# Another order of VectorE's step in layer one's attention, and feed-forward output products inside the feed-forward loop

## The chip, the cores and the metric

The kernel runs on one core of a Trainium2 chip. The metric is the device time of one execution in microseconds; lower is better.

## What is computed

A block of a network on 16 sequences of 32 tokens with 512 channels. First a graph attention over the 512 channels seen as points (two layers, windows of ten neighbours, four orderings), then a state-space mixing layer, then a gated feed-forward with repeated weights and low-rank adapters. The change touches the first layer of the graph attention and the feed-forward:

```python
scores = jnp.einsum('bihd,bjhd->bhij', qh, qh) / np.float32(np.sqrt(headdim))
attn = jax.nn.softmax(scores, axis=-1)
out = jnp.einsum('bhij,bjhd->bihd', attn, qh).reshape(B * N, k, total)
...
h1 = jnp.einsum('oc,bnkc->bonk', W_conv1, g1)
h1 = _lrelu(_instance_norm(h1, (2, 3)))
feats1 = h1.max(axis=-1)
...
def _qlora_linear(x, wq, A, B):
    w = jnp.tile(wq, (1, 4))
    return x @ w.T + (x @ A.T @ B.T) * LORA_SCALING
gate = jax.nn.silu(_qlora_linear(x, w1q, a1, b1))
up = _qlora_linear(x, w3q, a3, b3)
return _qlora_linear(gate * up, w2q, a2, b2)
```

## The kernel before

**Layer one's attention.** `windows_and_attention` builds the windows and then runs `steps(engine, step, T, U)` on each engine: T = 192 steps, a hardware loop whose body is U = 8 steps, with the steps ahead of it and behind it written out. `at(lag)` gives the item that a step handles with that lag, so in step k an engine works on items k-1, k-3 and so on. An item is 15 sub-windows of 3 points. Four items (SL = 4) make a pack, whose values are mixed together. What happens to an item, in order:

- TensorE `scores`: a mask product (L1564), then 15 times two products into `pQ` (L1569, L1571).
- ScalarE copies scores to `small`/`Sc` (L1672) and values to `Vs` (L1678), lag 1.
- VectorE takes the maximum `mx` (L1490), lag 1; GpSimd subtracts it, `Dm` (L1428), lag 1; ScalarE takes the exponential `E` (L1691), lag 2; VectorE sums it, `Z` (L1494), and inverts the sum, `R` (L1503), both lag 3; GpSimd multiplies, `A` (L1435), lag 3; VectorE transposes `A` to `AT` (L1499), lag 4.
- TensorE `mix`: once a pack, lag 5, four centre products (L1589) and 60 small products (L1594) into `pH`; it waits for the transposes of the whole pack.
- ScalarE copies the outputs to `Hs` with their sum (L1685) and squares them (L1697); VectorE takes the maximum over neighbours, `hmax` (L1509), all lag 6, once a pack.

The views name tiles by the memory that they lie in: `QT` is Dm, E or A, `onehot` is Vs, Hs or AT, `small` is Sc. Each engine runs its instructions in the order written. VectorE's order in a step is: maximum of k-1, sum of k-3, transpose of k-4, reciprocal of k-3, and once a pack the maximum over outputs of k-6. GpSimd's is: subtract of k-1, multiply of k-3.

**Feed-forward.** The hidden width is cut into 12 parts (HT), n = 0 to 11. For each n TensorE makes six products of 512 columns (`passes`, L2951), two adapter products of 6 rows (`adapters`, L2958) and then the two `low_rank` products of part n-1 (L2939, L2942). ScalarE makes the silu (L2827), VectorE the product with `up` (L2887), ScalarE its high half in 16 bits (L2831), VectorE its low half (L2892), on which the second `low_rank` product waits. GpSimd adds up the four parts that share a row of the repeated weight, `uf` (L2920); for each of three such sums r (FR = 3) ScalarE and VectorE make the high and low half `uf16` (L2834 and L2899, for r = 2 L2836 and L2901). VectorE also makes the low half of the output weights, `W2` (L2894). Behind the loop the output comes: for each of four blocks of tokens q nine products (three r by three pairs of halves, L2984) and one 4-row product in float32 with `la2` (L2986), then VectorE's `res` (L2907) and the store.

Of the kernel before, what the change touches and what calls it, by code (L numbers as in the profile page):

```python
# [6 lines left out]
F32 = mybir.dt.float32  # L7
# [3 lines left out]
ALU = mybir.AluOpType  # L11
# [1161 lines left out]
def windows_and_attention(nc, io, scratch, layer, O, feats, runs, perm, rank, fixed, W, hmax, stat, field):  # L1173
# [12 lines left out]
    with ExitStack() as ctx:  # L1186
# [143 lines left out]
        def valid(tile):  # L1330

            return tile.rearrange("p (s x) -> p s x", x=32)[:, :, 0:PTS * K]
# [109 lines left out]
        def _(dve):  # L1442
# [40 lines left out]
                                    rows(cen, k, 0, (1, PTS), (0, K), (PTS, 2)), ALU.subtract).then_inc(q_v, 1)  # L1483

            def step(k, at):
                if at(1):
                    (t, _), p = at(1), (k - 1) % ND
                    dve.wait_ge(scores_out, t + 3)
                    dve.wait_ge(shifted, t + 1)
                    v.tensor_reduce(mx[:, p, :], valid(Sc[:, p, :]), X, ALU.max).then_inc(max_ready, 1)  # L1490
                if at(3):
                    (t, _), p = at(3), (k - 3) % ND
                    dve.wait_ge(exped, t + 1 + ND)
                    v.tensor_reduce(Z[:, p, :], valid(E[:, p, :]), X, ALU.add).then_inc(summed, 1)  # L1494
                if at(4):
                    (t, r), k5 = at(4), (k - 4) % U
                    dve.wait_ge(probs, t + 1 + ND)
                    dve.wait_ge(mixed, pack(r, k5) + (RV - NA) // SL + 1)
                    v.transpose(AT[:, k5 % NA, :], A[:, k5 % ND, :]).then_inc(turned, 1)  # L1499
                if at(3):  # L1500
                    (t, _), p = at(3), (k - 3) % ND
                    dve.wait_ge(summed, t + 1)
                    v.reciprocal(R[:, p, :], Z[:, p, :]).then_inc(r_ready, 1)  # L1503
                if at(6) and (k - 6) % SL == SL - 1:
                    (_, r), k6 = at(6), (k - 6) % U
                    q, p = pack(r, k6), k6 // SL % 2
                    dve.wait_ge(copied, q + 3)
                    dve.wait_ge(squared, q + 3)
                    v.tensor_reduce(hmax[:, bass.ds(q * GP, GP)],  # L1509
                                    Hs[:, p, :].rearrange("p (n j) -> p n j", j=K), X, ALU.max).then_inc(hmax_done, 1)  # L1510

            steps(dve, gather_step, B, 4)
            steps(dve, step, T, U)
# [1181 lines left out]
def feed_forward(nc, io, scratch, P, out):  # L2695


    with ExitStack() as ctx:
# [8 lines left out]

        HT = 4 * FR
        LR = 38
        UP = 2.0 ** 10  # L2710
        ident = sb("ident_f", [128, 128])
        w13 = sb("w13_f", [128, 2, FFH])
# [29 lines left out]
        pl = ctx.enter_context(nc.psum_tensor("pl_f", [128, 512], F32))  # L2742
        pg = ctx.enter_context(nc.psum_tensor("pg_f", [128, 2, 512], F32))
        pu = ctx.enter_context(nc.psum_tensor("pu_f", [128, 2, 512], F32))
        i_in = sem("i_in_f")
        w_in = sem("w_in_f")
        a_in = sem("a_in_f")
# [36 lines left out]
        def turned_to(d):  # L2784

            return pt[:, d, :] if d < 2 else pu[:, d - 2, :]

        def u_of(n):

# [19 lines left out]
        @block.scalar  # L2809
        def _(act):  # L2810
            act.wait_ge(var_ready, 1)
            nc.scalar.activation(tmp[:, 0, :], mv[:, :, 1], ACT.Sqrt).then_inc(root_ready, 1)
            act.wait_ge(w_in, 32)
            nc.scalar.activation(W16[:, 0, 0, :], w13[:, 0, :], ACT.Copy, scale=UP).then_inc(w_high, 1)
            nc.scalar.activation(W16[:, 1, 0, :], w13[:, 1, :], ACT.Copy, scale=UP).then_inc(w_high, 1)
            act.wait_ge(b_in, 32)
            nc.scalar.activation(bh[:, :], b13[:, :], ACT.Copy, scale=UP).then_inc(b_high, 1)
            act.wait_ge(xf_ready, 1)
            nc.scalar.activation(X16[:, 0, :], xf[:, :], ACT.Copy).then_inc(x_high, 1)
            act.wait_ge(w2_in, 48)  # L2820
            nc.scalar.activation(A2[:, :, 0:2], a2[:, :, :], ACT.Copy, scale=UP).then_inc(w2_high, 1)
            nc.scalar.activation(W2[:, 0, :, :], w2[:, :, :], ACT.Copy, scale=UP).then_inc(w2_high, 1)
            for n in range(HT):
                act.wait_ge(gu_mm, n + 1)
                if n >= 2:
                    act.wait_ge(u_ready, n - 1)
                nc.scalar.activation(sg[:, n % 2, :], pg[0:FP, n % 2, :], ACT.Silu, scale=1.0 / UP).then_inc(silued, 1)  # L2827
                act.wait_ge(u_ready, n + 1)
                if n >= 2:
                    act.wait_ge(la2_mm, n - 1)  # L2830
                nc.scalar.activation(u16[:, n % 2, 0, :], u_of(n), ACT.Copy).then_inc(u_high, 1)  # L2831
                if n % 4 == 3 and n >= 4:
                    act.wait_ge(uf_ready, 3 * (n // 4))
                    nc.scalar.activation(uf16[:, 0, n // 4 - 1, :], uf[:, n // 4 - 1, :], ACT.Copy).then_inc(uf_high, 1)  # L2834
            act.wait_ge(uf_ready, 3 * FR)
            nc.scalar.activation(uf16[:, 0, FR - 1, :], uf[:, FR - 1, :], ACT.Copy).then_inc(uf_high, 1)  # L2836

        @block.vector
        def _(dve):
# [41 lines left out]
            for n in range(HT):  # L2881
# [8 lines left out]
                if n >= 2:  # L2890
                    dve.wait_ge(la2_mm, n - 1)
                v.tensor_tensor(u16[:, n % 2, 1, :], u_of(n), u16[:, n % 2, 0, :], ALU.subtract).then_inc(u_split, 1)  # L2892
                if n == 5:
                    v.scalar_tensor_tensor(W2[:, 1, :, :], w2[:, :, :], UP, W2[:, 0, :, :], ALU.mult, ALU.subtract)\  # L2894
                        .then_inc(w2_split, 1)
                if n % 4 == 3 and n >= 4:
                    r = n // 4 - 1
                    dve.wait_ge(uf_high, r + 1)
                    v.tensor_tensor(uf16[:, 1, r, :], uf[:, r, :], uf16[:, 0, r, :], ALU.subtract).then_inc(uf_split, 1)  # L2899
# [4 lines left out]
            v.tensor_scalar(la2[:, :], pl[0:4, :], 0.5, None, ALU.mult).then_inc(la2_ready, 1)  # L2904
            for q in range(TT):
                dve.wait_ge(out_mm, q + 1)
                v.scalar_tensor_tensor(res[:, q, :], (pg if q < 2 else pu)[:, q % 2, :], 1.0 / UP, x2[:, q, :],  # L2907
                                       ALU.mult, ALU.add).then_inc(res_ready, 1)

        @block.gpsimd  # L2910
# [13 lines left out]
        def _(pe):  # L2924
# [29 lines left out]
            def adapters(n):  # L2954
# [4 lines left out]
                                            L16[32 * i:32 * i + 6, :], start=False, stop=True)  # L2959
                last.then_inc(gu_mm, 1)  # L2960

            pe.wait_ge(x_split, 1)
            passes(0)
            passes(1)
# [6 lines left out]
            for n in range(2, HT):  # L2971
                pe.wait_ge(u_ready, n - 1)
                passes(n)
                adapters(n)
                low_rank(n - 1)
            low_rank(HT - 1)
            pe.wait_ge(w2_split, 1)
            pe.wait_ge(la2_ready, 1)
            pe.wait_ge(uf_split, FR)
            for q in range(TT):  # L2980
                po = (pg if q < 2 else pu)[:, q % 2, :]
                for r in range(FR):
                    for a, b in ((0, 0), (0, 1), (1, 0)):
                        nc.tensor.matmul(po, uf16[:, a, r, q * 128:(q + 1) * 128], W2[:, b, r, :],  # L2984
                                         start=r + a + b == 0, stop=False)
                nc.tensor.matmul(po, la2[:, q * 128:(q + 1) * 128], b2[:, :], start=False, stop=True).then_inc(out_mm, 1)  # L2986


# [118 lines left out]
```

## Time and profile before

| | us |
|---|---|
| median of three runs | 2203.59 |
| lowest and highest run | 2200.35, 3210.74 |
| the profiled execution | 2203.48 |
| its span in the trace | 2201.7 |

| engine | busy us | share of the span |
|---|---|---|
| TensorE | 1865.4 | 85% |
| VectorE | 1840.4 | 84% |
| ScalarE | 1596.5 | 73% |
| GpSimd | 1071.2 | 49% |

Layer one's attention steps run from about 268 to 676 us of the span, the feed-forward from about 2112 us to its end. The shares above are means over all stages; each stage has another limit, so the stages are read one by one. A row of the timeline gives the start, the duration, the engine, the line and the tiles of an instruction; two instructions of one engine may overlap by some hundredths, so what an instruction costs its engine is read from start to start.

### The profile page before, as it was taken

The page shows a single profiled execution, that of the slowest core. Times are in us where ns is not written, and L with a number is a line of the kernel's source. Part 1 is how long each engine was busy: PE and PEld are TensorE (multiplying, and loading weights), DVE is VectorE, ACT ScalarE, POOL GpSimd, SP SyncE. Part 2 cuts the span into 40 slices and gives each one's busy share as a digit, 9 for nine tenths or more (in the row PEclk, how much of TensorE's full clock was granted, in tenths as well). Part 3 has the DMA queues.
Part 4 walks back from the last instruction along what each step waited for, and adds up shares of the span by engine and source line. Part 5 has one row for each costly group of instructions (what it writes and reads, how often), then busy time and mean ns, then how long its engine had stood idle before and what let it go on. Part 6 is the DMA issues. An engine that isn't in the chain of part 4 may idle for free. (4 is left out here: it accounts for less than half of the span.)

```text
span 2201.7 us, 99587 instructions
## 1 busy us (share of the span) xinstructions
PE 1865.4 (85%) x37653; PEld 1274.8 (58%) x37656; DVE 1840.4 (84%) x3511; ACT 1596.5 (73%) x3296; POOL 1071.2 (49%) x1160
## 2 busy tenths in 40 slices
PE   4876688888885674899999994879999999999957
PEld 2333377777773333899999993424545554554522
DVE  8899889999995996799999996847888888888864
ACT  7899778888886996899999993565554554454432
POOL 1220189999992002687788771003445444544511
PEclk9976699999996666999999996999999999999977
DMA  1157865555551776545545531302222222222110
GB/s 37 37 122 175 187 140 126 121 120 127 119 110 34 177 175 159 108 105 110 108 105 108 110 83 45 92 27 91 82 86 76 81 86 79 83 81 86 48 51 20
DMA packets 434897, 215.53 MB, mean 98 GB/s; under 512 B 301196, under 2 KB 404268, under 8 KB 434681
## 3 DMA queue, kind: packets, MB, share of 16 engines
q1 hardware_dynamic: 431872, 212.24, 40.0%
q10 hardware_dynamic: 2936, 2.18, 0.4%
q8 instruction: 48, 0.79, 0.2%
q14 instruction: 41, 0.33, 0.0%
HBM read 161.35 MB, written 52.86 MB: 97 GB/s over the span
## 5 line engine op out<-in xcount | busy, mean ns | idle before, releaser
L1015 PE MATMUL pQ<-QM,QX 128*128 128x96 f16 x2880 | 299.6, 227 | 1.6 <-issue 1.6
L1013 PE MATMUL pQ<-neigh_lo,QX 128*128 128x64 f16 x2880 | 292.7, 195 | 3.3 <-issue 3.3
L1013 PEld LDWEIGHTS pQ<-neigh_lo,QX 128*128 128x128 f16 x2880 | 276.3, 103 | 3.1 <-issue 3.1
L1015 PEld LDWEIGHTS pQ<-QM,QX 128*128 128x128 f16 x2880 | 274.8, 103 | 2.1 <-issue 2.1
L2656 POOL TENSOR_TENSOR MT<-cb,decay 128x512 f32 (+1 forms) x128 | 174.8, 1386 | 207.7 <-DVE half L2567 152.5
L1571 PE MATMUL pQ<-QM,QX 128*128 128x64 f16 x2880 | 232.0, 206 | 0.0
L1569 PE MATMUL pQ<-neigh_lo,QX 128*128 128x32 f16 x2880 | 227.5, 182 | 0.0
L1569 PEld LDWEIGHTS pQ<-neigh_lo,QX 128*128 128x128 f16 x2880 | 218.9, 103 | 2.8
L1111 POOL TENSOR_TENSOR Dm<-Sc,mx 128x450 f32<-128x450 f32 x192 | 183.1, 954 | 71.5 <-DVE mx L1071 71.5
L1571 PEld LDWEIGHTS pQ<-QM,QX 128*128 128x128 f16 x2880 | 212.4, 104 | 0.3
L1435 POOL TENSOR_TENSOR QT<-QT,R 128x450 f32<-128x450 f32 x192 | 183.0, 953 | 37.1 <-DVE R L1503 28.2
L2624 DVE SCALAR_TENSOR_TENSOR cv_m<-pX,taps_m,cv_m 128x496 f32<-128x496 f32 (+2 forms) x192 | 137.6, 717 | 73.6 <-ACT cv_m L2530 55.9
L1118 POOL TENSOR_TENSOR Ap<-E,R 128x450 f32<-128x450 f32 x192 | 182.9, 952 | 30.6 <-DVE R L1084 29.4
L2671 POOL TENSOR_TENSOR sqsum<-sqsum,sq 128x512 f32<-128x512 f32 x56 | 83.0, 1483 | 231.2 <-ACT sq L2519 231.2
L1428 POOL TENSOR_TENSOR QT<-small,mx 128x450 f32<-128x450 f32 x192 | 182.7, 952 | 13.8 <-DVE mx L1490 13.8
L1148 ACT ACTIVATE Vs<-pQ 128x960 f32<-128x960 f32 x192 | 187.0, 974 | 0.0
L2535 ACT ACTIVATE hid<-cv_m 128x512 f32<-128x512 f32 x64 | 40.3, 630 | 198.3 <-DVE cv_m L2624 198.3
L2431 PE MATMUL pG<-h,W 128*128 128x512 f16 x768 | 178.5, 383 | 4.2 <-DVEq L2560 4.2
L2449 PE MATMUL pO<-Wo,yw 128*128 128x512 f16 x768 | 176.2, 379 | 1.6 <-DVE yw L2614 1.6
L2431 PE MATMUL pX<-h,W 128*128 128x512 f16 x768 | 176.2, 379 | 0.0
L1691 ACT ACTIVATE QT<-QT 128x450 f32<-128x450 f32 x192 | 112.2, 584 | 60.1 <-POOL QT L1428 60.1
L1499 DVE STREAM_TRANSPOSE onehot<-QT 128x480 f32<-128x480 f32 x192 | 129.8, 676 | 26.2 <-PE pH L1594 10.7
(455 smaller groups left out, 5221.9 us busy)
## 6 DMA issues: line engine op xcount, KB each, us to landing
QM<-scratch_q SPq DMA_DIRECT2D x192, 240.0 KB, 2.7
QX<-scratch_q SPq DMA_DIRECT2D x768, 60.0 KB, 2.3
scratch_q<-QT SPq DMA_DIRECT2D x124, 360.0 KB, 5.1
Wo<-in_out_proj SPq DMA_DIRECT2D x64, 256.0 KB, 2.6
Wg<-in_in_proj SPq DMA_DIRECT2D x62, 256.0 KB, 2.7
Wh<-in_in_proj SPq DMA_DIRECT2D x62, 256.0 KB, 2.8
W_s<-in_in_proj SPq DMA_DIRECT2D x20, 256.0 KB, 2.7
CT<-scratch_c SPq DMA_DIRECT2D x192, 11.2 KB, 2.1
```

What stands on the lines that cost most here:

```text
L1013: nc.tensor.matmul(pQ[:, p, u // PB, o + 32:o + BW], qx[u], W["neigh_lo"][:, 0:O], start=False, stop=True, skip_group_check=True)
L1015: last = nc.tensor.matmul(pQ[:, p, u // PB, o:o + BW], qx[u], qm[u], start=False, stop=True, skip_group_check=True)
L1111: nc.gpsimd.tensor_tensor(valid(Dm[:, p, :]), valid(Sc[:, p, :]), mx[:, p, :].unsqueeze(2).to_broadcast([128, SUBS, PTS * K]), ALU.subtrac ...
L1118: nc.gpsimd.tensor_tensor(valid(A[:, p, :]), valid(E[:, p, :]), R[:, p, :].unsqueeze(2).to_broadcast([128, SUBS, PTS * K]), ALU.mult).then ...
L1148: nc.scalar.activation(like(Vs[:, kv % RV, :], O, O), blocks(p, 32, O), ACT.Copy).then_inc(vs_ready, 1)
L1428: nc.gpsimd.tensor_tensor(valid(Dm[:, p, :]), valid(Sc[:, p, :]), mx[:, p, :].unsqueeze(2).to_broadcast([128, SUBS, PTS * K]), ALU.subtrac ...
L1435: nc.gpsimd.tensor_tensor(valid(A[:, p, :]), valid(E[:, p, :]), R[:, p, :].unsqueeze(2).to_broadcast([128, SUBS, PTS * K]), ALU.mult).then ...
L1569: nc.tensor.matmul(pQ[:, p, u // PB, o + 32:o + BW], qx[u], W["neigh_lo"][:, 0:O], start=False, stop=True, skip_group_check=True)
L1571: last = nc.tensor.matmul(pQ[:, p, u // PB, o:o + BW], qx[u], qm[u], start=False, stop=True, skip_group_check=True)
L2431: last = nc.tensor.matmul(out, W16[:, i, quarter, a, d, :], h16[:, b, d, :], start=d + a + b == 0, stop=d == DT - 1 and a == 1)
L2449: last = nc.tensor.matmul(pO[:, q, :], yw[:, k4 % 2, a, q * 128:(q + 1) * 128], Wo16[:, k4 % 2, b, :], start=k4 + a + b == 0, stop=k4 == U ...
L2656: nc.gpsimd.tensor_tensor(MT[:, k1 % 2, h, :, :].rearrange("p q (b i) -> p q b i", b=4), P["cb"][:, bass.ds(r, 1), :, :].rearrange("p g q ...
```

## The change

In layer one's attention VectorE's step gets another order: sum of k-3, maximum of k-1, reciprocal of k-3, once a pack the maximum over outputs, now of k-7, then the transpose of k-4. The maximum over outputs no longer waits for the square. Layer two's attention, a function of its own, stays.

In the feed-forward 24 of the 36 output products (those of r = 0 and 1) move from behind the loop into it, as eight pieces of three: five in the iterations 7 to 11 (`EARLY`), three between the loop and the last `low_rank`. For that the outputs lie in other banks, with one new one, `pr`. The halves of `uf` for r = 0 and 1 are made at n = 5 and 9 instead of 7 and 11, the low half of `W2` at n = 3 instead of 5.

```diff
             def step(k, at):
+                if at(3):
+                    (t, _), p = at(3), (k - 3) % ND
+                    dve.wait_ge(exped, t + 1 + ND)
+                    v.tensor_reduce(Z[:, p, :], valid(E[:, p, :]), X, ALU.add).then_inc(summed, 1)
                 if at(1):
...
                     v.tensor_reduce(mx[:, p, :], valid(Sc[:, p, :]), X, ALU.max).then_inc(max_ready, 1)
                 if at(3):
                     (t, _), p = at(3), (k - 3) % ND
-                    dve.wait_ge(exped, t + 1 + ND)
-                    v.tensor_reduce(Z[:, p, :], valid(E[:, p, :]), X, ALU.add).then_inc(summed, 1)
+                    dve.wait_ge(summed, t + 1)
+                    v.reciprocal(R[:, p, :], Z[:, p, :]).then_inc(r_ready, 1)
+                if at(7) and (k - 7) % SL == SL - 1:
+                    (_, r), k7 = at(7), (k - 7) % U
+                    q, p = pack(r, k7), k7 // SL % 2
+                    dve.wait_ge(copied, q + 3)
+                    v.tensor_reduce(hmax[:, bass.ds(q * GP, GP)],
+                                    Hs[:, p, :].rearrange("p (n j) -> p n j", j=K), X, ALU.max).then_inc(hmax_done, 1)
                 if at(4):
                     (t, r), k5 = at(4), (k - 4) % U
                     dve.wait_ge(probs, t + 1 + ND)
                     dve.wait_ge(mixed, pack(r, k5) + (RV - NA) // SL + 1)
                     v.transpose(AT[:, k5 % NA, :], A[:, k5 % ND, :]).then_inc(turned, 1)
-                if at(3):
-                    (t, _), p = at(3), (k - 3) % ND
-                    dve.wait_ge(summed, t + 1)
-                    v.reciprocal(R[:, p, :], Z[:, p, :]).then_inc(r_ready, 1)
-                if at(6) and (k - 6) % SL == SL - 1:
-                    (_, r), k6 = at(6), (k - 6) % U
-                    q, p = pack(r, k6), k6 // SL % 2
-                    dve.wait_ge(copied, q + 3)
-                    dve.wait_ge(squared, q + 3)
-                    v.tensor_reduce(hmax[:, bass.ds(q * GP, GP)],
-                                    Hs[:, p, :].rearrange("p (n j) -> p n j", j=K), X, ALU.max).then_inc(hmax_done, 1)
...
+        EARLY = {7: (0, 0), 8: (1, 0), 9: (2, 0), 10: (0, 1), 11: (1, 1)}
...
+        pr = ctx.enter_context(nc.psum_tensor("pr_f", [128, 512], F32))
...
+        def out_of(q):
+
+            return (pt[:, 0, :], pt[:, 1, :], pr[:, :], pg[:, 0, :])[q]
...
-                if n % 4 == 3 and n >= 4:
+                if n % 4 == 1 and n >= 4:
                     act.wait_ge(uf_ready, 3 * (n // 4))
                     nc.scalar.activation(uf16[:, 0, n // 4 - 1, :], uf[:, n // 4 - 1, :], ACT.Copy).then_inc(uf_high, 1)
...
-                if n == 5:
+                if n == 3:
                     v.scalar_tensor_tensor(W2[:, 1, :, :], w2[:, :, :], UP, W2[:, 0, :, :], ALU.mult, ALU.subtract)\
                         .then_inc(w2_split, 1)
-                if n % 4 == 3 and n >= 4:
+                if n % 4 == 1 and n >= 4:
...
+            def piece(q, r):
+
+                pe.wait_ge(uf_split, r + 1)
+                for a, b in ((0, 0), (0, 1), (1, 0)):
+                    nc.tensor.matmul(out_of(q), uf16[:, a, r, q * 128:(q + 1) * 128], W2[:, b, r, :],
+                                     start=r + a + b == 0, stop=False)
...
                 adapters(n)
+                if n == 7:
+                    pe.wait_ge(w2_split, 1)
+                if n in EARLY:
+                    piece(*EARLY[n])
                 low_rank(n - 1)
+            piece(2, 1)
+            pe.wait_ge(u_ready, HT - 1)
+            piece(3, 0)
+            piece(3, 1)
             low_rank(HT - 1)
-            pe.wait_ge(w2_split, 1)
-            pe.wait_ge(la2_ready, 1)
-            pe.wait_ge(uf_split, FR)
             for q in range(TT):
-                po = (pg if q < 2 else pu)[:, q % 2, :]
-                for r in range(FR):
-                    for a, b in ((0, 0), (0, 1), (1, 0)):
-                        nc.tensor.matmul(po, uf16[:, a, r, q * 128:(q + 1) * 128], W2[:, b, r, :],
-                                         start=r + a + b == 0, stop=False)
+                piece(q, FR - 1)
+                if q == 0:
+                    pe.wait_ge(la2_ready, 1)
+                po = out_of(q)
                 nc.tensor.matmul(po, la2[:, q * 128:(q + 1) * 128], b2[:, :], start=False, stop=True).then_inc(out_mm, 1)
```

## Rows read from the trace of the kernel before

**Rows 1.** Windows view, attention loop: stretch, us, busy (x instructions), clock, DMA

```profile
core 0: us, PE busy (x) PEld busy (x) DVE busy (x) ACT busy (x) POOL busy (x), PEclk, DMA share, GB/s
315.00:660.00 345.00, 294.26 (x10584) 270.53 (x10584) 322.88 (x713) 289.11 (x672) 312.97 (x336) 1.00 0.57 121
```

**Rows 2.** Timeline of VectorE over one pack: start, duration, engine, line, operation

```profile
453.78 0.68 DVE L1499 STREAM_TRANSPOSE onehot<-QT 128x480 f32<-128x480 f32 x1
454.39 0.21 DVE L1503 RECIPROCAL R<-Z 128x15 f32<-128x15 f32 x1
454.52 0.56 DVE L1509 TENSOR_REDUCE hmax<-onehot 128x450 f32 x1
455.00 0.61 DVE L1490 TENSOR_REDUCE mx<-small 128x15 f32<-128x450 f32 x1
455.52 0.61 DVE L1494 TENSOR_REDUCE Z<-QT 128x15 f32<-128x450 f32 x1
456.05 0.67 DVE L1499 STREAM_TRANSPOSE onehot<-QT 128x480 f32<-128x480 f32 x1
456.64 0.21 DVE L1503 RECIPROCAL R<-Z 128x15 f32<-128x15 f32 x1
...
457.99 0.68 DVE L1499 STREAM_TRANSPOSE onehot<-QT 128x480 f32<-128x480 f32 x1
...
460.05 0.68 DVE L1499 STREAM_TRANSPOSE onehot<-QT 128x480 f32<-128x480 f32 x1 [0.24 <-PE pH L1594]
...
462.01 0.68 DVE L1499 STREAM_TRANSPOSE onehot<-QT 128x480 f32<-128x480 f32 x1
```

**Rows 3.** Timeline of GpSimd in the same pack

```profile
454.76 0.95 POOL L1435 TENSOR_TENSOR QT<-QT,R 128x450 f32<-128x450 f32 x1
455.68 0.95 POOL L1428 TENSOR_TENSOR QT<-small,mx 128x450 f32<-128x450 f32 x1
457.01 0.95 POOL L1435 TENSOR_TENSOR QT<-QT,R 128x450 f32<-128x450 f32 x1 [0.37 <-DVE R L1503]
457.92 0.95 POOL L1428 TENSOR_TENSOR QT<-small,mx 128x450 f32<-128x450 f32 x1
```

**Rows 4.** Waits from 300 to 660 us: total us, times, longest

```profile
ACT QT L1691 <- POOL QT L1428: 56.1, 87, 0.8
PE pH L1594 <- DVE onehot L1499: 28.8, 43, 0.7
```

**Rows 5.** Timeline of ScalarE in the same pack

```profile
456.67 0.58 ACT L1691 ACTIVATE QT<-QT 128x450 f32<-128x450 f32 x1 [0.50 <-POOL QT L1428]
457.15 0.53 ACT L1672 ACTIVATE small<-pQ 128x450 f32<-128x450 f32 x1
```

**Rows 6.** Timeline of TensorE behind the feed-forward loop

```profile
2174.54 4.00 PE L2984 MATMUL pg_f<-W_f,uf_f 115*128 115x512 f16 x9 [1.26 <-DVE la_f L2904]
2178.47 2.07 PE L2986 MATMUL pg_f<-b_f,la_f 4*128 4x512 f32 x2
2180.47 4.02 PE L2984 MATMUL pg_f<-W_f,uf_f 115*128 115x512 f16 x9
...
2196.26 1.12 PE L2986 MATMUL pu_f<-b_f,la_f 4*128 4x512 f32 x2
```

**Rows 7.** Windows view: the feed-forward loop, and the products behind it

```profile
2144.90:2172.20 27.30, 21.84 (x91) 6.76 (x89) 18.84 (x22) 12.68 (x22) 10.14 (x8) 1.00 0.00 1
...
2175.60:2196.10 20.50, 20.50 (x40) 5.81 (x38) 2.07 (x3) 0.00 (x0) 0.00 (x0) 0.50 0.10 38
```

**Rows 8.** Timeline of TensorE in the feed-forward loop, iterations 9 and 11

```profile
2162.18 0.82 PE L2951 MATMUL pg_f<-X_f,W_f 128*128 128x512 f16 x3
...
2163.59 0.39 PE L2958 MATMUL pg_f<-L_f,B_f 6*128 6x512 f16 x1
...
2167.59 0.82 PE L2951 MATMUL pg_f<-X_f,W_f 128*128 128x512 f16 x3
```

**Rows 9.** Source view of L2892: durations in ns, by operands

```profile
L2892 DVE TENSOR_TENSOR u_f<-u_f x9: 1196/1199/1200, 2141.1 to 2171.4; 115x512 f16<-115x512 f32 x9
L2892 DVE TENSOR_TENSOR u_f<-uf_f,u_f x3: 692/693/693, 2139.1 to 2163.7; 115x512 f16<-115x512 f32 x3
```

**Rows 10.** Timeline of VectorE at the end of the feed-forward loop

```profile
2172.56 0.68 DVE L2899 TENSOR_TENSOR uf_f<-uf_f 115x512 f16<-115x512 f32 x1
2173.16 0.68 DVE L2901 TENSOR_TENSOR uf_f<-uf_f 115x512 f16<-115x512 f32 x1
2173.76 0.67 DVE L2904 TENSOR_SCALAR la_f<-pl_f 4x512 f32<-4x512 f32 x1
```

More of the change, by code:

```diff
@@ L2906, in _ @@
                 dve.wait_ge(out_mm, q + 1)
-                v.scalar_tensor_tensor(res[:, q, :], (pg if q < 2 else pu)[:, q % 2, :], 1.0 / UP, x2[:, q, :],
+                v.scalar_tensor_tensor(res[:, q, :], out_of(q), 1.0 / UP, x2[:, q, :],
                                        ALU.mult, ALU.add).then_inc(res_ready, 1)
```

## The prediction

> **What bounds the kernel now.** Only two stages are touched, so I read these and leave the rest alone. First the windows view of the attention loop: 345.00 us hold 168 steps (336 GpSimd instructions, two a step), 2.05 us each. VectorE is busy 322.88 us, GpSimd 312.97, TensorE 294.26, ScalarE 289.11 [rows 1]. No engine is full, so the limit is a ring through several of them, and the timelines show which. From one transpose to the next VectorE takes 2.27, 1.94, 2.06 and 1.96 us, 8.23 a pack [rows 2]. The reader should ask of each length whether VectorE's own work fills it.
>
> The 2.27 is full: transpose 0.61, reciprocal 0.13, maximum over outputs 0.48, maximum 0.52, sum 0.53, from start to start. Without the output maximum the sum is 0.60 + 0.13 + 0.48 + 0.53 = 1.74 (the first reduction of a row costs 0.48, the last 0.53). The other three steps are 0.20 to 0.32 longer than that. What fills them is a ring through GpSimd: the transpose holds the reciprocal back 0.59; the reciprocal at 456.64 lets the multiply start at 457.01, 0.37 later [rows 3]; the multiply lets the next transpose start at 457.99, 0.98 later. 0.59 + 0.37 + 0.98 = 1.94, just the step. The transpose at 460.05, the first of a pack, comes 0.10 later than the ring gives; its row names TensorE, but the buffer that it fills was freed a pack ago, so I keep 0.10 as a fixed cost of that one transpose.
>
> Then the feed-forward's end. Behind the loop TensorE runs four times nine products and a 4-row product in float32: 3.93 + 2.00 us a block [rows 6], from 2174.54 to 2197.4, 22.8 us (the last 4-row product took 1.12). From 2175.60 to 2196.10 it was busy 20.50 of 20.50 us and the granted clock was still 0.50, which is 1.2 GHz; in the loop before it was 1.00 [rows 7]. The clock had fallen while TensorE waited for the last part.
>
> **Attention: the new order.** Nothing is added; each instruction keeps its price. The reciprocal now stands in front of the transpose, so the ring transpose, reciprocal, multiply, transpose is gone: between a reciprocal and the transpose of its product now lie a transpose, a sum, a maximum and a reciprocal, 1.74 us, against the 1.35 that it needs. VectorE's own sum would be 3 x 1.74 + 2.27 = 7.49 a pack.
>
> But the maximum now comes second, and with it the subtract and, behind it on GpSimd, the multiply. Let z be the start of the sum. Maximum at z + 0.48. The subtract starts 0.68 behind the maximum (455.00 to 455.68 [rows 2, 3]; there GpSimd's multiply held it as well, so 0.68 is at most a little too long), so z + 1.16. The multiply follows 0.91 later (454.76 to 455.68 and 457.01 to 457.92 for the other way round, same shape), so z + 2.07, and the transpose of the next step can't start before z + 3.05, in the first of a pack z + 3.15. The transpose is wanted at z + 1.14 of its own step, with the output maximum at z + 1.67, and the next z is 0.60 behind it. So a step that follows one of length x has the length max(1.74, 3.65 - x); with the output maximum max(2.27, 3.65 - x); first of a pack max(1.74, 3.75 - x). The output maximum stands in step 2 of four (lag 7), the first-of-pack transpose in step 0. Going round: step 2 2.27; step 3 max(1.74, 1.38) = 1.74; step 0 max(1.74, 2.01) = 2.01; step 1 max(1.74, 1.74) = 1.74. Sum 7.76 against 8.23, so 0.47 less, 0.117 a step. GpSimd alone would need 4 x 1.82 = 7.28.
>
> What hides the others: ScalarE waits 56.1 us for the subtract [rows 4]; its exponential starts 0.99 behind the subtract, the copy for the maximum 0.48 later [rows 3, 5], and that copy is wanted at the next but one maximum, so 1.16 + 0.99 + 0.48 + about 0.6 = 3.2 against 3.96; the pack's two longer ScalarE steps take 0.5 of the slack and leave some. TensorE waits 28.8 us in 43 packs for the last transpose [rows 4], 0.67 each, besides a wait on ScalarE, so it has a little over the 0.47 that is to be cut. If that cover were gone, it would be TensorE that holds the pack, at 8.23 - 0.67 = 7.56 by this wait alone. The output maximum reads a copy made one ScalarE step earlier and is one step later than before: no wait; the square's wait is dropped and cost nothing in a steady pack. No DMA is moved. Of 48 packs the first four are held by filling and I count 44: 44 x 0.47 = 20.7 us. Bounds: 0, and 44 x 0.74 = 32.6 if only VectorE's sum holds.
>
> By the Trainium skill ("SBUF — State Buffer", Who interferes with whom) a VectorE instruction with two SBUF inputs is blocked by a GpSimd one that reads SBUF, one with a single input is not. The trace agrees for the first: the low half beside GpSimd's sum takes 1199 ns, otherwise 693 [rows 9]. That rule speaks for unchanged prices in the attention.
>
> **Feed-forward.** 24 of 36 products leave the end. What stays per block: three products, 3.93 / 3 = 1.31, and the 4-row one, 2.00, at 1.2 GHz; 0.65 and about 1.1 at 2.4 GHz (1.12 [rows 6]). Four blocks: 13.2 or 7.0 us, against 22.8. Which clock: the pieces fill the hole in which it fell before, so it begins high; but more than half of what stays are the 4-row products, and with them in between the clock stayed low for 20 us of full work. I take the middle, 10.1 us, both ends for the range: -12.7 (-9.6 to -15.8).
>
> By the Trainium skill ("TensorE: Matmul & The Clock Gate", Part 1) sustained matmul work releases the throttle; then this end would run high and the sum be 3.1 better. The trace does not agree: 20.5 us of full work at 0.50.
>
> The start of the end: the low half L2899 no longer stands ahead of L2901 (0.60 from start to start, of which the wait for ScalarE's half, ready about 2172.8, leaves 0.4), and the `la2` step (2173.76 to 2174.54) is now hidden behind three products: -1.0 [rows 6, 10].
>
> In the loop five pieces are added, three products each: six take 1.41 [rows 8], so 0.65 to 0.70. TensorE stands idle 27.30 - 21.84 = 5.5 us over some ten iterations [rows 7], 0.55 each, the waits for the low half. Iterations are 2.70 on average (2162.18 to 2167.59). A piece stands ahead of that wait and is nearly covered: 5 x 0.15 = 0.7. In iteration 10 piece (0, 1) waits for the low half made at n = 9, which comes 0.6 behind the half that `low_rank` waits for, so this and the piece itself (1.3) lie on the path: +1.3. The three pieces behind the loop (2.0) lie in the wait for the last part (silu to low half, over 3 us). `W2`'s low half and the `uf` halves only move. Sum +2.0; bounds 0 and 4. The stage: -12.7 - 1.0 + 2.0 = -11.7, between -17 and -7.
>
> **Sum.** -20.7 - 11.7 = -32.4 against the profiled execution, 2203.48 (span 2201.7 and 1.8 around it), which is within 0.1 of the median of the runs: 2171.1 us, 1.5% less. A measurement of this kernel tells about 2% from no change, so this is "within 2%", the border being 2159.5.
>
> **The rivals.**
>
> - VectorE alone holds the attention (7.49): -32.6 - 11.7 gives 2159, with a high clock at the end 2156. For it: 0.68 may be too long. Against: GpSimd's chain of 3.65 in two steps is made of prices seen many times. 0.17.
> - A new wait eats over half of the gain: the maximum is late for GpSimd, or TensorE, whose spare is small, holds the pack at 7.9 to 8.1. -8 - 11.7 gives 2184. For it: TensorE's thin cover. 0.20.
> - The order does nothing for the time, as one ring takes the place of the other at 8.23: 2192. It needs the two-step chain of 3.65 to be 4.1. 0.07.
> - Slower: in the new order transposes run beside GpSimd's reads and are held as L2892 is, +0.51 each: 7.49 + 2.04 = 9.53 a pack, 44 x 1.3 = +57, and with the feed-forward +45: 2249. It decides from 0.19 a transpose on. Against: today transposes already overlap both GpSimd instructions and take 0.67 or 0.68 [rows 2, 3]. 0.04.
>
> **How the numbers follow.** The forecast has 0.52. The range 2155 to 2188 takes in both clock bounds, the first rival's middle and the second's, and leaves out the last two and the edges. Its own range is 2163 to 2177. Faster by over 2%: most of the first rival and a little of the forecast's edge, 0.17; slower 0.04; the rest 0.79.
>
> **What would show it.** Steps of a pack at about 2.27, 1.74, 2.0, 1.74; GpSimd's wait for R (L1435) gone and waits for the maximum in its place; 8.23 falling to 7.8. In the feed-forward twelve products of r = 2 behind the loop, the end 7 to 13 us long by its clock, the loop about 2 us longer. I am wrong if TensorE's wait for the transpose falls to nothing while the pack stays over 7.9, if a transpose takes over 0.7, or if the iterations with pieces grow by a full 0.65 each.

## The result: 2165.1 us, and the profile after

| | before | after |
|---|---|---|
| median of the runs, us | 2201.97 | 2165.11 |
| lowest and highest of the undisturbed runs | 2193.99, 2203.59 | 2161.28, 2167.82 |
| span of the profiled execution | 2201.7 | 2164.4 |
| layer one's windows and attention, us | 572.1 | 548.5 |
| feed-forward, us | 89.9 | 78.1 |

The ratio is 0.9837, 95% interval 0.9811 to 0.9863: 1.6% less, within the 2% that counts as the same. (One run of the kernel before, 3210.74 us, was disturbed and is left out of the ratio; 2201.97 is the median with it, 2200.35 without.) The predicted 2171.1 is 6 us above, and 2165.11 lies in both ranges. The profiled spans differ by 37.3 us: 23.6 in layer one, 11.8 in the feed-forward, 1.4 in layer two, whose code is the same in every kernel here and whose length goes from 475.7 to 480.1 in their traces, the rest elsewhere.

VectorE's timeline over a pack of the changed kernel. L1489 is the sum (Z), L1494 the maximum (mx), L1498 the reciprocal (R), L1503 the maximum over outputs, L1509 the transpose:

```profile
450.03 0.68 DVE L1509 STREAM_TRANSPOSE onehot<-QT 128x480 f32<-128x480 f32 x1 [0.20 <-PE pH L1593]
...
451.81 0.62 DVE L1509 STREAM_TRANSPOSE onehot<-QT 128x480 f32<-128x480 f32 x1
452.36 0.57 DVE L1489 TENSOR_REDUCE Z<-QT 128x15 f32<-128x450 f32 x1
452.86 0.60 DVE L1494 TENSOR_REDUCE mx<-small 128x15 f32<-128x450 f32 x1
453.38 0.24 DVE L1498 RECIPROCAL R<-Z 128x15 f32<-128x15 f32 x1
453.53 0.56 DVE L1503 TENSOR_REDUCE hmax<-onehot 128x450 f32 x1
454.01 0.66 DVE L1509 STREAM_TRANSPOSE onehot<-QT 128x480 f32<-128x480 f32 x1
...
455.10 0.61 DVE L1494 TENSOR_REDUCE mx<-small 128x15 f32<-128x450 f32 x1
455.62 0.24 DVE L1498 RECIPROCAL R<-Z 128x15 f32<-128x15 f32 x1
455.78 0.62 DVE L1509 STREAM_TRANSPOSE onehot<-QT 128x480 f32<-128x480 f32 x1
...
457.79 0.68 DVE L1509 STREAM_TRANSPOSE onehot<-QT 128x480 f32<-128x480 f32 x1 [0.21 <-PE pH L1593]
```

From transpose to transpose: 1.78, 2.20, 1.77, 2.01 us, in sum 7.76, where [rows 2] gave 2.27, 1.94, 2.06, 1.96. Between 451.81 and 454.01 and in the step behind it each instruction starts where the one before it lets it: VectorE's own sum. Only the step that ends at 457.79 has a hole, and GpSimd's timeline says why (L1428 subtract, L1435 multiply):

```profile
454.55 0.95 POOL L1435 TENSOR_TENSOR QT<-QT,R 128x450 f32<-128x450 f32 x1
455.78 0.95 POOL L1428 TENSOR_TENSOR QT<-small,mx 128x450 f32<-128x450 f32 x1 [0.28 <-DVE mx L1494]
456.69 0.96 POOL L1435 TENSOR_TENSOR QT<-QT,R 128x450 f32<-128x450 f32 x1
```

Maximum 455.10, subtract 455.78 (0.68 later), multiply 456.69 (0.91 later), transpose 457.79 (1.10 later). This is the chain that the prediction had drawn. In [rows 3] GpSimd waited for the reciprocal; now it waits for the maximum.

The windows view and the waits from 300 to 620 us (L1690 is ScalarE's exponential, L1593 TensorE's small products):

```profile
315.00:640.00 325.00, 292.56 (x10560) 269.53 (x10557) 316.15 (x713) 284.21 (x671) 309.01 (x335) 1.00 0.59 128
```

```profile
ACT QT L1690 <- POOL QT L1428: 39.9, 81, 0.8
...
POOL QT L1428 <- DVE mx L1494: 13.6, 42, 2.0
PE pH L1593 <- DVE onehot L1509: 8.7, 40, 0.2
```

325 us now hold 335 GpSimd instructions against 336 in 345 us [rows 1], and VectorE is busy 97% of the stretch against 94%. TensorE's wait for the pack's last transpose fell from 0.67 to 0.22 us each [rows 4]: it was the cover, and 0.45 of it is used up.

TensorE behind the feed-forward loop (L2971 pieces, L3002 the 4-row products), and the windows view of two stretches of it:

```profile
2149.59 0.82 PE L2971 MATMUL pt_f<-W_f,uf_f 115*128 115x512 f16 x3 [0.30 <-DVE uf_f L2906]
2150.34 1.12 PE L3002 MATMUL pt_f<-b_f,la_f 4*128 4x512 f32 x2
2151.39 0.82 PE L2971 MATMUL pt_f<-W_f,uf_f 115*128 115x512 f16 x3
2152.14 1.12 PE L3002 MATMUL pt_f<-b_f,la_f 4*128 4x512 f32 x2
2153.20 1.43 PE L2971 MATMUL pr_f<-W_f,uf_f 115*128 115x512 f16 x3
2154.56 2.07 PE L3002 MATMUL pr_f<-b_f,la_f 4*128 4x512 f32 x2
2156.56 1.46 PE L2971 MATMUL pg_f<-W_f,uf_f 115*128 115x512 f16 x3
2157.95 2.07 PE L3002 MATMUL pg_f<-b_f,la_f 4*128 4x512 f32 x2
```

```profile
2149.60:2153.20 3.60, 3.60 (x11) 1.00 (x11) 1.21 (x2) 0.00 (x0) 0.00 (x0) 1.00 0.03 13
2153.40:2160.00 6.60, 6.60 (x10) 1.43 (x8) 1.29 (x2) 0.00 (x0) 0.00 (x0) 0.50 0.27 101
```

Two blocks at 2.4 GHz, 1.80 each, and two at 1.2 GHz, 3.4 each: 10.43 us in place of 22.84. TensorE was busy without a gap in the 3.6 us before the fall and in the 6.6 us after it.

### The profile page after: what moved, and what is told of

It is laid out like the page before. It is cut to its first block and busy times, and to the rows that moved or that the text cites. A ratio compares the mean times of both kernels' runs of the same rounds, so it can differ in the third digit from the quotient of the medians.

```text
span 2164.4 us, 99543 instructions
## 1 busy us (share of the span) xinstructions
PE 1853.2 (86%) x37656; PEld 1269.9 (59%) x37656; DVE 1833.2 (85%) x3511; ACT 1592.1 (74%) x3296; POOL 1068.8 (49%) x1160
## 5 line engine op out<-in xcount | busy, mean ns | idle before, releaser
L1428 POOL TENSOR_TENSOR QT<-small,mx 128x450 f32<-128x450 f32 x192 | 183.5, 956 | 30.9 <-DVE mx L1494 26.2
L1435 POOL TENSOR_TENSOR QT<-QT,R 128x450 f32<-128x450 f32 x192 | 184.2, 960 | 0.7 <-DVE R L1498 0.7
L1690 ACT ACTIVATE QT<-QT 128x450 f32<-128x450 f32 x192 | 113.2, 590 | 46.1 <-POOL QT L1428 46.0
L1080 DVE STREAM_TRANSPOSE AT<-Ap 128x480 f32<-128x480 f32 x192 | 129.3, 674 | 7.3 <-POOL Ap L1118 1.6
```

What stands on the lines that cost most here:

```text
L1428: nc.gpsimd.tensor_tensor(valid(Dm[:, p, :]), valid(Sc[:, p, :]), mx[:, p, :].unsqueeze(2).to_broadcast([128, SUBS, PTS * K]), ALU.subtrac ...
L1435: nc.gpsimd.tensor_tensor(valid(A[:, p, :]), valid(E[:, p, :]), R[:, p, :].unsqueeze(2).to_broadcast([128, SUBS, PTS * K]), ALU.mult).then ...
```

## The experiments

The stage lengths below were read alike from all traces: us a pack as the mean of 40 packs; the feed-forward as three lengths, from the first to the last silu (loop), from there to the first product behind the loop (start), and from there to the end of the last product (end). "Block" is the whole of layer one's windows and attention.

| kernel | us a pack | block | loop + start + end | median, us |
|---|---|---|---|---|
| before | 8.229 | 572.1 | 32.31 + 5.11 + 22.84 | 2201.97 |
| after | 7.769 | 548.5 | 34.01 + 4.11 + 10.43 | 2165.11 |
| attention_only | 7.762 | 546.7 | 31.84 + 5.11 + 14.10 | 2173.98 |
| ffn_only | 8.23 | 571.4 | 33.61 + 4.11 + 8.28 | 2188.86 |
| order_only | 8.552 | 586.4 | 32.29 + 5.11 + 22.82 | 2219.14 |
| hmax_only | 8.234 | 570.6 | 31.83 + 5.11 + 14.09 | 2189.95 |
| max_first | 8.378 | 577.1 | 33.53 + 4.11 + 8.39 | 2189.57 |
| order_lag6_no_square | 7.862 | 552.7 | 34.06 + 4.11 + 10.38 | 2169.57 |
| order_lag7_square | 7.763 | 547.9 | 33.62 + 4.10 + 8.26 | 2165.44 |
| lag8_bias_last | 7.755 | 547.7 | 33.60 + 4.11 + 6.65 | 2163.26 |
| lag8_late_pieces | 7.755 | 547.6 | 32.05 + 4.48 + 10.42 | 2166.05 |
| combined | 7.758 | 547.4 | 32.45 + 4.48 + 7.74 | 2163.37 |
| after_again | 7.762 | 548.3 | 33.62 + 4.11 + 8.28 | 2167.52 |
| after_third | 7.762 | 548.5 | 33.62 + 4.11 + 8.30 | 2165.43 |

The first four experiments ran on one chip beside 15 runs of the kernel before (median 2192.52), the next four beside 7 (2199.83), the last four beside 9 (2194.65). Where one run stands for a kernel, a difference of a few us in its time says nothing, and the lengths in its trace carry the verdict. Lengths of the same code differ between traces by up to 1.8 us for the block (546.7 to 548.5 with the new order at lag 7) and by 0.4 to 0.5 us for the loop.

**The two stages apart.** `attention_only` has the attention part of the diff alone, with the feed-forward as before, `ffn_only` the feed-forward part alone.

> The attention's part of the change on the kernel before, feed-forward as before. If the two parts simply add, the attention stage gives back about 23 us (steps of a pack 2.20, 1.77, 2.01, 1.78, 7.77 us a pack as in the changed kernel), so about 2179 us against 2202. Rival, part of the difference of the two kernels is elsewhere, as the stages between seemed 2 us shorter too: those 2 us stay away or come here, which would give 2177 or 2181.

> The feed-forward's part alone, attention as before. Adding up: 11.8 us less, about 2190 us; the end behind the loop 10.4 us with two blocks at 2.4 GHz and two at 1.2 GHz. Rival, the clock at the end depends on where the end falls in time: the fall comes earlier or later by a block, and the end takes anything from 7 to 13 us.

Attention alone: 2173.98 us, ratio 0.9902 (0.9871 to 0.9934), about 21 us less by the ratio and 18.5 by the medians. Feed-forward alone: 2188.86 us, ratio 0.9983 (0.9963 to 1.0002): by this comparison nothing certain. Its trace has an end of 8.28 us, shorter than the 10.4 expected and inside what the rival allowed. Much of the reason is in the clock of the other side. `attention_only` runs the very code of [rows 6], and this is its end:

```profile
2148.84 3.75 PE L2983 MATMUL pg_f<-W_f,uf_f 115*128 115x512 f16 x9 [1.47 <-DVE la_f L2903]
2152.53 1.12 PE L2985 MATMUL pg_f<-b_f,la_f 4*128 4x512 f32 x2
2153.58 2.12 PE L2983 MATMUL pg_f<-W_f,uf_f 115*128 115x512 f16 x9
```

```profile
2148.80:2152.10 3.30, 3.26 (x8) 1.20 (x9) 0.00 (x0) 0.00 (x0) 0.00 (x0) 0.50 0.00 0
2152.30:2165.80 13.50, 10.65 (x37) 3.56 (x35) 2.76 (x4) 0.00 (x0) 0.00 (x0) 1.00 0.21 78
```

Here the clock, low at first as in [rows 7], came back to 2.4 GHz at the end of the first nine products and stayed: nine products in 2.12 us, not 4.02, and an end of 14.10 us, not 22.84. So the old end has two lengths, 8.7 us apart, and which of them a run gets isn't in the code. The times of the kernel before fall into two groups that fit the two lengths, 9.2 us apart from first silu to last product (60.26 and 51.05): of its 34 undisturbed runs in the four sets of this study 19 lie from 2189.1 to 2194.7 us and 15 from 2199.7 to 2205.2, none in between, with a mean granted clock of 0.916 to 0.921 in the lower group and 0.912 to 0.916 in the upper one in the three later sets. `attention_only` splits likewise, 2168.1 to 2171.1 and 2176.9 to 2179.9. That each group has its own end rests on few traces: the one kept of the kernel before, with the long end, is of the upper group (2203.48 us), the one kept of `attention_only`, with the short end, of its lower one (2169.08). Compared group with group, attention alone gives 21 to 23 us. The feed-forward's gain is 11.7 us against the long end (60.26 to 48.55, first silu to last product) and 5.0 against the short one, with the clock of the new end high for most of it (51.05 to 46.01 in `after_again`).

That does not settle `ffn_only`: against the lower group of its own set alone (ten runs, median 2190.4) its median is 1.5 us less, not 5.0. Its ten runs spread from 2183.8 to 2194.6 us, and the trace kept is of the shortest. Where the others lose the rest stays open.

**The parts of the attention.** In `order_only` VectorE's order is the new one, but the maximum over outputs stays at lag 6 with its wait for the square, and the feed-forward is the old one. `hmax_only` is the reverse: the old order, with lag 7 and no wait for the square (the same lines the other way round, in the kernel before).

```diff
 # order_only, against the changed kernel
-                if at(7) and (k - 7) % SL == SL - 1:
+                if at(6) and (k - 6) % SL == SL - 1:
...
                     dve.wait_ge(copied, q + 3)
+                    dve.wait_ge(squared, q + 3)
```

> The new order of VectorE's step, but the maximum over outputs still of k-6 and still waiting for the square. By my rings the order alone is worth little: the square ends about 3.4 us behind the start of the sum of the step before, the output maximum would be wanted 3.0 behind it, so VectorE stands 0.4 to 0.5 us there once a pack, and the lengths are 2.75, 1.74, 1.91, 1.84: 8.1 to 8.3 us a pack, no gain. Rival, the order is all and the place of the output maximum incidental: 7.77 us a pack, 2179 us.

> The old order, only the maximum over outputs of k-7 instead of k-6 and without the wait for the square. The ring transpose, reciprocal, multiply, transpose stays: one step of 2.27 and three of 1.94 to 2.06, 8.23 us a pack, no gain beyond some 2 us in the first packs, where it waited for the square. Rival, the output maximum's wait was what held the packs: under 8.0.

Neither part pays. `hmax_only` changed nothing (8.234 us a pack), as expected. The new order alone made a pack 0.32 us slower than before, the block 14 us longer: no gain, as expected, but outside the 8.1 to 8.3, as the step with the maximum over outputs took 2.95 us where 2.75 stood. VectorE's timeline of `order_only` and two of its waits show what holds it:

```profile
450.76 0.24 DVE L1498 RECIPROCAL R<-Z 128x15 f32<-128x15 f32 x1
451.55 0.62 DVE L1504 TENSOR_REDUCE hmax<-onehot 128x450 f32 x1 [0.55 <-ACT junk L1697]
452.09 0.67 DVE L1510 STREAM_TRANSPOSE onehot<-QT 128x480 f32<-128x480 f32 x1
```

```profile
...
POOL QT L1428 <- DVE mx L1494: 42.7, 38, 2.8
...
DVE hmax L1504 <- ACT junk L1697: 20.0, 37, 0.6
```

The square (L1697) is late for an instruction that now stands ahead of the transpose. In the old order the maximum over outputs came last in its step, and there the same wait cost nothing (8.229 us a pack with it, 8.234 without). Two more kernels put back one of the two edits each, `order_lag6_no_square` with `at(6)` and without the wait, `order_lag7_square` with `at(7)` and with it.

> The changed kernel, but the maximum over outputs stays at lag 6; its wait for the square stays away. It tells which of the two edits of that instruction makes the new order pay (with neither of them a pack took 8.55 us, with both 7.77). Theory: the square is what is late; the copy of the outputs ends about 0.5 us ahead of the place that the maximum over outputs has in the step, so without the square there is no wait even at lag 6. Going round with the maximum over outputs in the step behind the first of a pack, the chain through GpSimd (multiply, subtract, multiply) gives 7.85 us a pack (transpose to transpose about 2.27, 1.74, 1.92, 1.92) and a time of about 2169 us. Rival: the copy is late as well; then VectorE's maximum over outputs waits, on ScalarE's L1684 copy, and a pack takes 8.2 to 8.55 us, the time 2185 to 2200 us.

> The changed kernel with the wait of the maximum over outputs for the square put back, at lag 7. Theory: one step later the square has ended more than a us ahead, the wait costs nothing, 7.77 us a pack and 2163 to 2168 us. Rival: the square slips with ScalarE's other work in a quicker step and is still late; then the wait shows on VectorE, a pack takes 8.0 us or more and the time is 2175 us or more.

Both came as the theory had them. Without the square, lag 6 gives 7.862 (transpose to transpose 2.26, 1.77, 1.90, 1.93): the wait for the square cost 0.69 us a pack, and the lag by itself is worth 0.09. With lag 7 the square is there in time, 7.763. So either edit makes the new order pay, and of the two together the wait's removal adds nothing that shows.

**Another order.** `max_first` keeps everything of the change but has the maximum ahead of the sum, as in the old order, so that GpSimd's subtract could start 0.5 us earlier.

```diff
                 if at(1):
                     ...
                     v.tensor_reduce(mx[:, p, :], valid(Sc[:, p, :]), X, ALU.max).then_inc(max_ready, 1)
+                if at(3):
+                    (t, _), p = at(3), (k - 3) % ND
+                    dve.wait_ge(exped, t + 1 + ND)
+                    v.tensor_reduce(Z[:, p, :], valid(E[:, p, :]), X, ALU.add).then_inc(summed, 1)
```

> The changed kernel with the maximum ahead of the sum. The subtract then starts 0.5 us earlier and the chain over GpSimd no longer holds the transpose, but the reciprocal stands right behind its sum, and the only such pair in the trace of the kernel before has 0.65 us between the starts instead of 0.53. VectorE's own work then sets the pack: three times 1.86 and 2.39 with the output maximum, 7.96 us. Rival: the reciprocal loses nothing behind its sum, and the pack is VectorE's 7.49 to 7.66.

8.378 us a pack, not the 7.96 expected and slower even than before the change. Three steps take 1.87 to 1.90, near the 1.86 expected; the one with the maximum over outputs takes 2.72 instead of 2.39. Its timeline:

```profile
449.58 0.62 DVE L1490 TENSOR_REDUCE mx<-small 128x15 f32<-128x450 f32 x1 [0.21 <-ACT small L1671]
450.12 0.61 DVE L1494 TENSOR_REDUCE Z<-QT 128x15 f32<-128x450 f32 x1
450.77 0.25 DVE L1498 RECIPROCAL R<-Z 128x15 f32<-128x15 f32 x1
```

Two things go wrong. Once a pack the earlier maximum meets ScalarE's score copy (L1671), which isn't ready. And the reciprocal, now right behind the sum whose result it waits for, starts 0.65 behind it, in the other three steps 0.63 to 0.64. In the changed kernel the maximum starts 0.50 behind the sum and the reciprocal 0.52 behind the maximum, and nothing is waited for. Sum first thus serves twice: it gives ScalarE time, and it puts another reduction between the sum and the reciprocal that waits for it.

**One step later still, and the end's order.** `lag8_bias_last` takes the maximum over outputs at lag 8 and makes the four float32 products with `la2` together behind all pieces. `lag8_late_pieces` has lag 8 and moves piece (0, 1) from iteration 10 to 11 and (1, 1) behind the loop:

```diff
-                if at(7) and (k - 7) % SL == SL - 1:
+                if at(8) and (k - 8) % SL == SL - 1:
...
-        EARLY = {7: (0, 0), 8: (1, 0), 9: (2, 0), 10: (0, 1), 11: (1, 1)}
+        EARLY = {7: (0, 0), 8: (1, 0), 9: (2, 0), 11: (0, 1)}
...
+            piece(1, 1)
             piece(2, 1)
```

> The changed kernel once more, on the chip of the kernels it is compared with. Theory: the feed-forward's end has two faces in the kernel before (90 us and 79 us, by the clock that it meets), and between 74 and 78 in the changed one; the attention is 23 us shorter always. Against the faster face the whole change is worth 27 to 28 us, against the slower 35. Rival: the 36 us of the first comparison come back whatever the clock, about 2165 against 2202.

> The changed kernel with two edits. Attention: maximum over outputs of k-8, so that its long step stands right ahead of the step with the first transpose of a pack, whose wait it then covers. By the rings the lengths are 2.27, 1.74, 1.91, 1.74 from there, 7.66 us a pack against 7.77, 4 to 5 us in all. Rival: VectorE's work is the same, so its place in the pack makes no difference, 7.77. Feed-forward: behind the loop first the twelve products of all four blocks, then the four 4-row products. If the clock falls because of the 4-row products, the twelve and at least one or two of the four run at 2.4 GHz and the end takes 7 to 9 us in every run; if it falls at a set time after the loop whatever runs, 9 to 10.5. Together 2157 to 2161 where the changed kernel has 2165.

> Attention as in the kernel with k-8: 7.66 us a pack, or 7.77 by the rival. Feed-forward: no piece in iteration 10, where piece (0, 1) waited 0.92 us for the half made just before; the later ones move one place, four behind the loop. If that wait is on the path, iteration 10 falls from 3.99 to about 2.5 us and the first product behind the loop comes 1.0 to 1.3 us earlier after the start of the stage; rival, the four pieces behind the loop now hold the last low_rank products and give it all back, 0 to 0.3.

`after_again`, the changed kernel once more: 2167.52, ratio 0.9861 (0.982 to 0.9902), and an end of 8.28 us, shorter than the 10.43 above as the clock fell only in the last block. Against the upper group of the kernel before in this set (four runs, median 2203.05) that is 35.5 us less, as expected, against the lower one (three runs, 2192.31) 24.8, short of the expected 27 to 28. `lag8_bias_last`: 2163.26, above the 2157 to 2161 expected, ratio 0.9842 (0.9803 to 0.9881). Its end took 6.65 us, 1.6 less, and in that run all of the 115-row products and most of the others had 2.4 GHz. But the clock fell 6.00 us behind the first of these products, and in `after_again`, with the float32 products in between, 6.06 us: putting them last did not hold the fall off. It left less work for the low clock. In the attention 7.755 us a pack is no gain over 7.762, where the rule of the prediction gives 7.66. That rule is what failed: it lets the subtract start 0.68 behind the maximum and leaves out that it also waits for GpSimd's own last multiply, 0.91 in front of it. Going round with both conditions gives 7.76 for lag 7, 7.84 for lag 6 and 7.74 for lag 8, against 7.769, 7.862 and 7.755 measured.

`lag8_late_pieces` took 1.6 to 2.0 us off the loop, 32.05 against 33.6 to 34.0 in the runs of the changed kernel: iteration 10 shrinks from 3.99 to 2.42 us, as this wait of the changed kernel is gone:

```profile
2142.36 0.82 PE L2971 MATMUL pt_f<-W_f,uf_f 115*128 115x512 f16 x3 [0.92 <-DVE uf_f L2904]
```

0.4 of it comes back in the start, as four pieces fill the hole behind the loop; 1.2 us are left, as expected.

**All three together.** `combined` has lag 8, the late pieces and the float32 products last.

> The changed kernel with three more edits, each of which took time away in one look or one comparison before: maximum over outputs at lag 8; the piece (0, 1) in iteration 11 and (1, 1) behind the loop; the float32 products with la2 together behind all others. Theory: they add up: a pack 7.75 us, the feed-forward loop from first to last silu 32.05 us (33.6 to 34.0 in the changed kernel), the products behind the loop 6.65 us; so 0.8 + 1.5 + 1.6 us or more off the changed kernel, 2159 to 2162 us where that gives 2163 to 2167. Rival 1: what the late pieces save in the loop comes back in the wait of the last low-rank products, as the three to four pieces behind the loop fill the hole: then only 1.6 to 2.4 us are left. Rival 2: with fewer products in the loop TensorE's clock falls ahead of the end, the last products run at 1.2 GHz (about 10 us instead of 6.65) and the time is that of the changed kernel, within 1 us.

> The changed kernel as it is, beside the combined one on the same chip, so that the two can be compared, and once more for its ratio to the kernel before. Expected 2163 to 2168 us; the feed-forward's products behind the loop take 8.28 or 10.43 us, by how many of their blocks TensorE's clock is high for, the loop from first to last silu 33.6 to 34.0 us. Rival: a third length of the end, which would mean that the clock's two outcomes don't describe it.

2163.37 us, outside the 2159 to 2162 expected, against 2165.43 for the changed kernel on the same chip (ratios 0.985, 0.9822 to 0.9879, and 0.9861, 0.9834 to 0.9888): not to be told apart. `after_third` came as expected, with a loop of 33.62 and an end of 8.30. First silu to last product it is 44.67 us against 46.03, but `lag8_bias_last`, without the late pieces, has 44.36. The clock took the rest, by the windows of `combined`:

```profile
2152.00:2154.00 2.00, 2.00 (x7) 0.83 (x6) 0.13 (x1) 0.00 (x0) 0.00 (x0) 1.00 0.00 0
2154.00:2156.00 2.00, 2.00 (x5) 0.84 (x4) 1.25 (x2) 0.00 (x0) 0.00 (x0) 0.73 0.28 103
2156.00:2157.70 1.70, 1.70 (x3) 0.18 (x1) 0.69 (x1) 0.00 (x0) 0.00 (x0) 0.50 0.54 198
```

It fell during the float32 products, with TensorE never idle, and its end took 7.74 us. So the second rival came in part: 1.1 of what is saved is lost again. That fewer products in the loop are the cause isn't shown: in `after`, with all of them in it, the clock fell 3.7 us behind the first product of the end, here 4.9.

The loop of 32.45 is 0.4 over that of `lag8_late_pieces`, and the traces show where that goes. Early in the loop the clock is at 1.2 GHz for a while in both kernels. In `combined` it is back at 2.4 GHz 7.7 us behind the first silu, in `lag8_late_pieces` 6.3, and the whole 0.4 lies in the first five lengths from silu to silu. The same holds in every trace kept: with the clock back after 7.7 to 7.8 us (`before`, `order_only`, `after`, `order_lag6_no_square`, `combined`) the loop is 0.4 to 0.5 us longer than in a kernel of the same feed-forward that has it back after 6.0 to 6.3. Compared like with like, the late pieces save 1.6 us both times. No version beats the changed kernel by more than the runs can show.

## Why the prediction was right, and where it was off

- **What bounds the attention, and the ring that goes**: right. The wait of GpSimd for the reciprocal is gone, the wait for the maximum stands in its place (13.6 us in 42 waits), and no transpose takes over 0.68 us, so the longer transposes of the fourth rival didn't come.
- **The length of a pack**: 7.76 predicted, 7.769 measured, with the steps 2.27, 1.74, 2.01, 1.74 as 2.20, 1.77, 2.01, 1.78. The 0.68 from maximum to subtract, which I had called a little too long, measured 0.68. The rule itself left out GpSimd's own order of work; this changed nothing at lag 7 (7.76 with it) and would have been 0.1 off at lag 8.
- **The cover on TensorE**: I put it at 0.67 a pack with 0.47 of it to go; 0.22 is left. The second rival, which lived on this, did not come.
- **"The square's wait is dropped and cost nothing in a steady pack"**: true of the kernel before, and `hmax_only` confirms it. I didn't ask what it would cost in the new order. At lag 6 that is 0.69 a pack, 30 us in 44 packs, which made the attention slower than before (`order_only`, the block 14.3 us longer); at lag 7 it is nothing (`order_lag7_square`). So the gain stood on either of two edits that I had both costed at nothing.
- **The number of packs**: the sum took 44 x 0.47 = 20.7 and nothing for the rest; measured 23.6. Steady packs give 18.9 (41 x 0.46), the filling 2.7 (first to 24th transpose 51.2 to 48.5), the last packs and the end 2. The filling and draining steps gain as well, which I had put at nothing; how much is known only roughly, as that first stretch takes 47.6 to 49.0 us in the four traces with this attention. This term was 3 us short.
- **The feed-forward's loop**: +2.0 predicted, +1.7 in the profiled pair (32.31 to 34.01). The wait in iteration 10, which I priced at 1.3 with its piece, is 0.92 and the iteration grew from 2.82 to 3.99, 1.17. The other pieces were priced too low: iterations 8 and 9 grew by 0.50 and 0.41 us, not by 0.15, though not by a full 0.65 either. What made up for it is iteration 7, which has a piece too and shrank from 3.52 to 3.10; I had counted nothing for moving the half of `uf` out of it, the likely reason, but no run moved it alone. Its start: -1.0 predicted, 5.11 to 4.11 measured, though the two parts that I named for it, 0.4 and 0.78, add up to 1.2.
- **The feed-forward's end**: 10.1 predicted, 10.43 in the profiled run. The two sides of the middle that I took, 13.2 and 7.0, are not reached: the clock begins high and falls on the way, in the last block or for the last two (8.3 or 10.4). The 10.1 was the middle of two bounds and not a reading of when the clock falls, so that it met 10.43 is luck: of seven other traces of these products in this order two have 10.38 and 10.42, five 8.26 to 8.39. That the old end has a second length besides 22.8 us I did not know; the profile that I had showed only the long one. The sum of -11.7 is right for this pair of traces (60.26 to 48.55) and too large by 6.7 for a run with the short end. With before's runs at 2192.52 in the median, as on another chip, the same change moves less; the ratios of three sets, 0.9837, 0.9861 and 0.9861, hold both kinds of runs.
- **The sum**: of the 4.9 us between -32.4 and the -37.3 of the two traces, 2.9 are the filling and end of the attention, 0.1 the feed-forward, and 1.9 lie in stages that the change does not touch.

## What to carry to other kernels

Where every engine has holes, read a step from start to start and ask of each length whether the engine's own work fills it; what doesn't is a ring or a wait. Here the reorder paid where it took a handoff out of the ring without putting another wait in (7.77 us a pack), and lost where it put one in (8.55). A wait that costs nothing where it stands has to be priced again at the place that its instruction gets: one and the same wait for the square was free behind the transpose, cost 0.69 us a pack ahead of it, and was free again one step later. And for an end that is all matmuls, look at several runs before pricing it, as its clock alone can be worth more than the edit.

## What the runs showed of the hardware

The granted clock of TensorE differed between runs of the same instructions. The old end ran wholly at 1.2 GHz in one trace (20.5 us without a gap, [rows 7]) and came back to 2.4 GHz in its first block in another. In `after` and in `combined` it fell from 2.4 to 1.2 GHz while TensorE had no gap, both times in a stretch where the 4-row float32 products took more than half of the time (1.05 of 1.80 us a block in `after`, start to start). Yet with these products last it fell 6.00 us behind the first product (`lag8_bias_last`) and with them in between 6.06 us (`after_again`). What decides stays open; no run here changed one thing of it alone. The Trainium skill ("TensorE: Matmul & The Clock Gate", Part 1) says that sustained matmul work releases the throttle, and that how many matmuls run at the low clock can differ between runs of one kernel. The second agrees with the two groups of times, the first does not agree with the 20.5 us.

A VectorE reciprocal that waits for the sum right in front of it starts 0.63 to 0.65 us behind it (`max_first`), while with another reduction between them there is no wait. And where GpSimd's multiply holds the first transpose of a pack, this starts 1.09 to 1.10 us behind the multiply's start, where the others that are held so start 0.98 to 0.99 behind (`before`, `hmax_only`, `order_only`, `order_lag6_no_square`); its row names TensorE, though the buffer that it fills was freed a pack ago. Why stays open.
